# Instance norm in a conv block: centring and leaky ReLU done by ScalarE straight from PSUM

## What is computed

```python
residual = x
out = conv2d(x, conv1_w, conv1_b, PAD)
mu = jnp.mean(out, axis=(2, 3), keepdims=True)
var = jnp.var(out, axis=(2, 3), keepdims=True)
out = (out - mu) * jax.lax.rsqrt(var + EPS)
out = jnp.where(out >= 0, out, NEG_SLOPE * out)      # NEG_SLOPE = 0.2
out = _refine(out, conv2_w, conv2_b, mask_w, mask_b, q_w, q_b, k_w, k_b, v_w, v_b)
return residual + out
```

## Time and profile before

| | |
|---|---|
| median of three runs | 212.4 us |
| span of the profiled execution, first to last instruction | 210.1 us |
| that execution's own time | not given apart; the median lies 2.3 us above the span |
| TensorE busy (granted clock 0.989 on the mean) | 184.5 us, 88% |
| DVE busy | 161.3 us, 77% |
| ScalarE busy | 119.4 us, 57% |
| GpSimd busy | 70.5 us, 34% |

### The profile page before, as it was taken

The page is one execution under the profiler, slowest core; times in us unless marked ns, Lnnn a source line. Parts: engine busy times, 40 slices in busy tenths (PEclk is TensorE's granted clock), DMA queues, the critical chain, the costliest instruction groups (busy, mean ns, idle before and its releaser), DMA issues.

```text
span 210.1 us, 5374 instructions
## 1 busy us (share of the span) xinstructions
PE 184.5 (88%) x2158; PEld 104.0 (50%) x2167; DVE 161.3 (77%) x382; ACT 119.4 (57%) x251; POOL 70.5 (34%) x62
## 2 busy tenths in 40 slices
PE   1799879879986999899997999899799998899972
PEld 1349339333353756643576455743423345565741
DVE  6798799988768859599497986994928576992682
ACT  2175273655259461967692862775845583966850
POOL 7600803150310403660007613750044003670290
PEclk9999999978999999999999999999999999999998
DMA  6412031001501000001000040001001000000002
GB/s 199 80 57 58 2 100 50 3 0 37 163 0 50 3 5 10 3 3 39 0 3 0 3 147 13 6 3 46 4 6 47 3 0 10 8 5 8 5 2 103
DMA packets 10154, 6.75 MB, mean 32 GB/s; under 512 B 7248, under 2 KB 8496, under 8 KB 10128
## 3 DMA queue, kind: packets, MB, share of 16 engines
q1 hardware_dynamic: 9888, 5.82, 10.2%
q10 hardware_dynamic: 240, 0.58, 0.7%
HBM read 3.30 MB, written 1.05 MB: 21 GB/s over the span
## 4 chain that ended last, share of the span: by engine, by line
PE 53%; DVE 22%; ACT 12%; issue 5%; DMA 3%; POOL 1%; SPq 1%; DVEq 0%; ACTq 0%
PE ps L1455 20%; PE ps L1375 5%; PE ps L1368 5%; PE ps L1402 5%; PE ps L1498 4%; ACT xw L703 3%; ACT p_t L720 3%; DVE sh_in L316 3%; PE ps L1533 3%; DMA w3b<-in_w_gi 2%; ACT sh_x L608 2%; PE ps L1544 2%; DVE ln_out L968 2%; PE ps L1522 2%; PE ps L1587 2%
## 5 line engine op out<-in xcount | busy, mean ns | idle before, releaser
L1455 PE MATMUL ps<-sh_ln,w_gi 96*64 96x512 f32 x192 | 44.6, 615 | 1.7 <-DVE sh_ln L316 1.7
L473 POOL TENSOR_TENSOR ln_s<-ln_s,neg_half 128x16 f32<-128x16 f32 x7 | 20.4, 2909 | 55.5 <-DVE ln_s L947 55.5
L608 ACT ACTIVATE sh_ln<-ln_out 32x512 f32<-32x512 f32 (+2 forms) x46 | 25.6, 557 | 14.6 <-DVE ln_out L968 5.5
L1455 PEld LDWEIGHTS ps<-sh_ln,w_gi 96*64 96x64 f32 x192 | 15.4, 140 | 25.9 <-issue 25.8
L1402 PE MATMUL ps<-w_qk,sh_ln 128*128 128x128 f32 x192 | 23.2, 278 | 0.4 <-issue 0.4
L1402 PEld LDWEIGHTS ps<-w_qk,sh_ln 128*128 128x128 f32 x192 | 22.2, 192 | 1.9 <-DMA sh_ln<-ln_out 0.9
L1498 PE MATMUL ps<-sh_in,w_in 96*32 96x256 f32 x384 | 22.8, 380 | 0.0
L1368 PE MATMUL ps<-busy 128*128 128x512 bf16 x68 | 19.4, 419 | 1.3 <-issue 1.2
L608 ACT ACTIVATE sh_x<-x 32x496 f32<-32x496 f32 (+1 forms) x20 | 12.3, 616 | 9.2 <-DVE x L1093 9.0
L1498 PEld LDWEIGHTS ps<-sh_in,w_in 96*32 96x32 f32 x384 | 11.9, 109 | 10.3 <-issue 3.0
L498 POOL TENSOR_TENSOR omm<-ones,msk 128x512 f32<-128x512 f32 x4 | 7.1, 1780 | 22.6 <-DVE msk L1169 22.6
(11 more groups left out here) (142 smaller groups left out, 334.6 us busy)
## 6 DMA issues: line engine op xcount, KB each, us to landing
sh_ln<-ln_out SPq DMA_DIRECT2D x27, 64.0 KB, 2.1
x_res<-in_x SPq DMA_DIRECT2D x4, 256.0 KB, 2.8
out_x<-out_s SPq DMA_DIRECT2D x4, 256.0 KB, 2.0
x_norm<-in_x SPq DMA_DIRECT2D x3, 256.0 KB, 2.9
kc<-in_shape_consts ACTq DMA_DIRECT2D x1, 450.0 KB, 4.9
w3b<-in_w_gi SPq DMA_DIRECT2D x1, 288.0 KB, 5.0
x_norm<-in_x SPq DMA_DIRECT2D x2, 128.0 KB, 2.8
xm<-xm SPq DMA_DIRECT2D x8, 25.5 KB, 1.9
```

What stands on the lines that cost most here:

```text
L473: nc.gpsimd.tensor_tensor(ln_s[n][:, 3, :], ln_s[n][:, 2, :], neg_half[:, :], ALU.pow)\
L608: return nc.scalar.activation(o, i, ACT.Copy)
L1455: mm = nc.tensor.matmul(ps[EC * h:EC * h + EC, GI_BANKS[n], :], w_gi[:, dy, n % 2, :], xs[:, n // 2, y:y + H // 2, 0:W], start=(dy == 0), ...
```

## The change

ScalarE no longer copies conv1's result to SBUF. It waits until DVE has the mean, then reads PSUM and writes the rectified activation `act_c` in one instruction per image: Prelu(PSUM + offset) with slope 0.2, the offset being bias - (mean + bias), a new small DVE instruction (`I_OFFSET`). DVE's `center` and its `lrelu` are gone, as are the buffers `hn` and `hc`.

```diff
-        g_c1_sb = signal("conv1_in_sbuf", 1)
-        g_in = signal("inorm_steps", 7)
+        g_in = signal("inorm_steps", 8)
-        g_act = signal("conv1_centered", 1, start=1)
-        g_lr = signal("lrelu_done", 1, start=1)
+        g_lr = signal("lrelu_done", 2, start=1)
...
-            def conv1_evac(pair, early=False):
-                act.wait_ge(g_in.sem, g_in.at(pair, 1))
-                act.wait_ge(g_act.sem, g_act.before(pair))
-                nc.scalar.activation(hc[:, :, :].rearrange("p i m -> p (i m)"), ps[:, conv1_bank(early), :],
-                                     ACT.Identity, bias=vec[:, V_BC1:V_BC1 + 1]).then_inc(g_c1_sb.sem, 1)
+            def lrelu(pair, early=False):
+                act.wait_ge(g_in.sem, g_in.at(pair, 5))
+                act.wait_ge(g_c2.sem, g_c2.before(pair))
+                if not is_first(pair):
+                    act.wait_ge(g_sc.sem, g_sc.done(pair - 1))
+                act.wait_ge(planes_by["in"]["dve"].sem, planes_by["in"]["dve"].before(pair))
+                for i in range(2):
+                    nc.scalar.activation(act_c[:, i, :], ps[:, conv1_bank(early), BLK * i:BLK * i + BLK], ACT.Prelu,
+                                         bias=inorm_v[:, I_OFFSET, i:i + 1], alpha=SLOPE).then_inc(g_lr.sem, 1)
...
                 dve.wait_ge(g_avg.sem, g_avg.at(pair, 1))
+                nc.vector.tensor_scalar(inorm_v[:, I_MEAN, :], ps[:, average_bank(early), 0:2],
+                                        vec[:, V_BC1:V_BC1 + 1], None, ALU.add).then_inc(g.sem, 1)
+                dve.wait_ge(g.sem, g.at(pair, 4))
+                nc.vector.tensor_scalar(inorm_v[:, I_OFFSET, :], inorm_v[:, I_MEAN, :], -1.0, vec[:, V_BC1:V_BC1 + 1],
+                                        ALU.mult, ALU.add).then_inc(g.sem, 1)
                 nc.vector.tensor_tensor(inorm_v[:, I_SHIFT, :], st[:, :, 0], ps[:, average_bank(early), 0:2],
-                                        ALU.subtract)\
-                  .then_inc(g.sem, 1)
-                nc.vector.tensor_scalar(inorm_v[:, I_MEAN, :], ps[:, average_bank(early), 0:2],
-                                        vec[:, V_BC1:V_BC1 + 1], None, ALU.add)\
-                  .then_inc(g.sem, 1)
-                dve.wait_ge(g.sem, g.at(pair, 4))
+                                        ALU.subtract).then_inc(g.sem, 1)
+                dve.wait_ge(g.sem, g.at(pair, 6))
...
-            def center(pair):
-
-                dve.wait_ge(g_c1_sb.sem, g_c1_sb.done(pair))
-                dve.wait_ge(g_in.sem, g_in.at(pair, 5))
-                dve.wait_ge(g_lr.sem, g_lr.before(pair))
-                for i in range(2):
-                    ins = nc.vector.tensor_scalar(hn[:, i, :], hc[:, i, :], inorm_v[:, I_MEAN, i:i + 1], None,
-                                                  ALU.subtract)
-                ins.then_inc(g_act.sem, 1)
-
...
-            def lrelu(pair):
-
-                dve.wait_ge(g_c2.sem, g_c2.before(pair))
-                dve.wait_ge(g_act.sem, g_act.done(pair))
-                planes_read("in", pair)
-                nc.vector.scalar_tensor_tensor(out=flat(act_c[:, :, :]), in0=flat(hn[:, :, :]), scalar=SLOPE,
-                                               in1=flat(hn[:, :, :]), op0=ALU.mult, op1=ALU.max)\
-                  .then_inc(g_lr.sem, 1)
...
             def average_var(pair, early=False):
                 avg = kc[:, K_AVG:K_AVG + P]
-                pe.wait_ge(g_in.sem, g_in.at(pair, 6))
+                pe.wait_ge(g_in.sem, g_in.at(pair, 7))
```

More of the change, by code:

```diff
@@ L68 @@
 SLOTS = D + 3
-I_MEAN, I_SHIFT, I_MOMENT, I_WAIT, I_BLOCK_VAR, I_VAR, I_RSTD = range(7)
+I_MEAN, I_SHIFT, I_MOMENT, I_WAIT, I_BLOCK_VAR, I_VAR, I_RSTD, I_OFFSET = range(8)
 class Signal:
@@ L160, in build @@
         gi = sb("gi", [P, 2, BANK])
-        hn = sb("hn", [P, 2, BLK])
-        hc = sb("hc", [P, 2, BLK])
         st6 = sb("st6", [P, 2, 6])
         st = sb("st", [P, 2, 2])
-        inorm_v = sb("inorm_v", [P, 7, 2])
+        inorm_v = sb("inorm_v", [P, 8, 2])
         th = sb("th", [P, 2 * BLK])
@@ L476, in inorm_rstd @@
             def inorm_rstd(pair):
-                pool.wait_ge(g_in.sem, g_in.at(pair, 7))
+                pool.wait_ge(g_in.sem, g_in.at(pair, 8))
                 nc.gpsimd.tensor_tensor(inorm_v[:, I_RSTD, :], inorm_v[:, I_VAR, :], neg_half[:, 0:2], ALU.pow)\
@@ L747, in step @@
                     squares(1, pair + 1)
-                conv1_evac(pair)
+                lrelu(pair)
                 qk_t_evac(pair + 2, 0)
@@ L813, in _ @@
             gelu(last, 0)
-            conv1_evac(but_last)
+            lrelu(but_last)
             in_planes(but_last)
@@ L820, in _ @@
             out1_evac(but_last)
-            conv1_evac(last, True)
+            lrelu(last, True)
             q_evac(but_last)
@@ L1238, in step @@
                 inorm_mean(pair)
-                center(pair)
                 variance(pair)
-                lrelu(pair)
                 in_planes(pair)
@@ L1317, in _ @@
             inorm_mean(but_last)
-            center(but_last)
             variance(but_last)
-            lrelu(but_last)
             in_planes(but_last)
@@ L1328, in _ @@
             inorm_mean(last, True)
-            center(last)
             variance(last, True)
-            lrelu(last)
             in_planes(last)
```

## The result

The changed kernel takes 210.38 us, the median of four executions (209.51, 210.25, 210.51 and 213.05), against 212.36 for four of the kernel before: a ratio of 0.989, 95% interval 0.9859 to 0.992. The forecast was 211.8. The profiled execution took 210.51 us, with a span of 208.3. All ratios and intervals leave out executions more than 1.5% above the fastest of the same kernel; the medians hold them.

What follows compares the result with a forecast made beforehand. The chain of waits was read as 53% TensorE and 22% DVE. Pair 1's -0.70 and pair 3's +0.14, with pairs 0 and 2 at zero, gave -0.56 us on 212.4, say 211.8, range 211.2 to 212.8.

Steps and rivals of the forecast that it cites:

- I add the sum to the median: Whole kernel: the summed change of -0.56 us, from the profiled execution's durations, is added to the median of 212.4 us.
- what can be told from no change: Whole kernel: three runs lie 0.4 us apart, so about 0.2%, or 0.42 us, can be told from no change.
- 2.3 us above that: Whole kernel: the median, 212.4 us, lies 2.3 us above the profiled 210.1 us from first to last instruction.
- Pair 0: First instance norm: worth nothing, covered by TensorE's V matmuls up to 74.99 and ScalarE's copies; without them 0.72 us.
- Pair 1: Second instance norm: 0.72 us earlier down to the halo; keys 0.67 to 0.72 earlier, taken as 0.70.
- The term for the first copy: DVE in every pair: the first `sh_in` copy could start where `lrelu` started, 114.48 instead of 115.20, 0.72 us less.
- Pair 2: Third instance norm: the moment comes about 0.33 us later within 0.36 of room; 0 to 0.1 us, taken as 0.
- Pair 3: Last instance norm: Prelus delay `k_h` and tanh by 0.33 us, tanh releases `msk`, `xm` 0.14 later.
- the slow rival: ScalarE: each Prelu takes y us more than 0.47; a loss from y = 0.22, 213.4 us at y = 0.47; chance 0.10.
- pair 3 doesn't lose: Last pair: if ScalarE catches up, `xm` comes 0.21 us earlier; sum -0.93, time 211.5 us; chance 0.12.
- The keys in pair 1 don't come earlier: Second pair: filler matmuls, halo DMA or DVE's layer norm lose the 0.70 or half; 212.2 to 212.5 us; chance 0.20.

Runs made afterwards that it cites:

- before_copy: The kernel before run once more, no edit: 211.56 us, median of 12, ratio 1.0038 to the kernel before beside it.
- fill_old_pair3: On the changed kernel with 9 filler matmuls, the last pair alone gets back the old evacuation, centring and leaky ReLU: 210.33 us, ratio 0.9914.
- fill_one_offset: On the changed kernel with 9 filler matmuls, the Prelu's offset taken straight from PSUM, without DVE's mean instruction: 209.52 us, ratio 0.9883.
- fill_both: On the changed kernel with 9 filler matmuls, pair 2's queries ahead of pair 3's Prelus and the offset straight from PSUM: 209.87 us, ratio 0.9881.
- after_fill: The changed kernel with 9 instead of 2 filler matmuls ahead of the first gate convolution: 210.15 us, ratio 0.995; a second time 210.56, ratio 0.9955.
- fill_q_first: On the changed kernel with 9 filler matmuls, ScalarE evacuates pair 2's queries ahead of pair 3's Prelus: 209.63 us, ratio 0.9881.

## Why the prediction was wrong

- **The step that failed** is the one that set the sum against the median: "I add the sum to the median", with 0.42 us as "what can be told from no change". It took the stretch ahead of the first instance norm as common to both kernels. In it lay a clock drop of 1.70 us, which the executions of one kernel have or don't have. The page of before had shown it (7 and 8 in the clock's row, mean 0.989), and I read over it. That all four executions of before (211.72 to 212.72) lay above the later median of 211.46, and three of the four of the changed kernel at 210.51 or below, was the luck of the draw. Three runs within 0.4 us of each other were no measure: 98 executions of that kernel (the first comparison's, those beside the series, and before_copy) spread from 209.27 to 215.32.
- **A term put at nothing** stands in the same step: the sum is one of the span, and adding it to the median takes what lies outside the span, "2.3 us above that", as unchanged. It grew by 0.35 us, from 1.81 to 2.16.
- **Direction**: faster was forecast. Inside the span the change is faster, by 0.31 us in the traces to DVE's end and by 0.39 in the spans of 24 against 24 executions. In the device time nothing is left of it, -0.04 with 0.34 either way.
- **Pair 0**: nothing, as forecast.
- **Pair 1**: forecast 0.70, measured 0.60. The mechanism was right, and the halo still released the keys. The term for the first copy was over-sized: I let it start where the leaky ReLU started, 0.12 us behind `variance`; it starts 0.20 behind (112.81 to 113.01). The halo's DMA took 1.92 instead of 1.88.
- **Pair 2**: forecast 0 of a bound of 0.1, measured 0.09. The offset took 0.23 us, not 0.17, and the moment's end came 0.39 us later against conv1, not 0.33: more than the 0.36 us of room.
- **Pair 3**: forecast +0.14, measured +0.14, by the path forecast: `k_h` 0.33 late, tanh late, `msk` released by tanh. The traces with the old form and with the queries first show that it is ScalarE's order. That this pair came out to the hundredth is luck in part: `act_in`'s start came 0.63 us earlier, not 0.72, which cost nothing since tanh was later still.
- **Rivals**: the Prelu costs what the slope of the Identity rows gave, 470 ns, so the slow rival was out; so was "pair 3 doesn't lose". "The keys in pair 1 don't come earlier" was out too. None of them was about the clock, and the largest gain among them was 0.93 us.

## What to carry to other kernels

Before a change of well under 1% is forecast or judged, look at the clock's row of the page and compare stretches between equal events in two traces; a difference ahead of the first changed instruction is not the change's. Compare the span and the time outside it separately: here one took back what the other gave. Work taken off the busiest non-bounding engine is worth something only in the stretch where the chain runs over it; here it paid in one pair of four. In another the chain ran over it too, but ScalarE, late for the same change, took its place. And where a copy that needed nothing is replaced by an instruction that waits for a statistic, what stands behind it in the queue is late: move the work that is ready ahead of it.

## What the runs showed of the hardware

TensorE's clock fell to 0.50, 1.2 GHz, after an idle stretch of only 1.73 us in two of four traces, and was granted in full after the same stretch in the other two; with 0.21 to 0.31 us of idle time instead it held there in all ten. The Trainium skill says in TensorE: Matmul & The Clock Gate, Part 1, that at a kernel's start the clock is run-variable, the same kernel coming out differently from one execution to the next. What the four traces show is the same in the middle of a kernel: TensorE's program ahead of the stretch is the same in all four, and only its times differ, by up to 1.10 us at the first gate convolution.

TensorE also took from 1.79 to 2.39 us for the same 24 matmul records of conv2 in pair 3, at a granted clock of 1.00 in every one of the fourteen traces. In four of the fourteen traces an "issue" of 0.16 to 0.30 us splits them behind the 14th. Why was not tried, and stays open.

The device time outside the span differs from kernel to kernel and hardly within one: 1.75 to 1.86 us for the old form, fill_old_pair3, fill_one_offset and fill_both, 2.11 to 2.21 for the changed kernel, after_fill and fill_q_first. That also stays open.
